# Attention and the last stage in one block, output bias written ahead, loads of the last stage on a new schedule

## The reference

```python
x = L0_attn_x                                    # (4, 2048, 512), f32
# attention: 16 heads of 32, on the normalised x
q = xn @ Wq.T + bq + ocr_bias; k = xn @ Wk.T + bk; v = xn @ Wv.T + bv
scores = einsum('bhsd,bhtd->bhst', q, k) / sqrt(32) + band   # band: 0.1 where |s - t| <= 2
x = x + (softmax(scores) @ v) @ Wo.T + bo
# last stage: both operands of the product go through an fp6 grid, in blocks of 32 along K
out = quantised(layernorm(x)) @ quantised(weight).T + bias
x = x + out
```

## Time and profile before

| | us |
|---|---|
| median of 3 runs | 4258.18 (4256.25 to 4260.35) |
| profiled execution | 4247.55 |
| its span, first to last instruction | 4245.8 |

### The profile page before, as it was taken

The page is one execution under the profiler, slowest core; times in us unless marked ns, Lnnn a source line. Parts: engine busy times, 40 slices in busy tenths (PEclk is TensorE's granted clock), DMA queues, the critical chain, the costliest instruction groups (busy, mean ns, idle before and its releaser), DMA issues. The chain is left out here.

```text
span 4245.8 us, 60060 instructions
## 1 busy us (share of the span) xinstructions
PE 4096.3 (96%) x21392; PEld 2549.3 (60%) x21392; DVE 3324.0 (78%) x5623; ACT 2406.2 (57%) x4652; POOL 3055.4 (72%) x1111
## 2 busy tenths in 40 slices
PE   8999989999999999999999999999999999949999
PEld 6888855555555555555555555555555555417777
DVE  5444449888888888888888888888888888617776
ACT  2222215766766677667666676666766677623221
POOL 2111116888889898989989889888888888935552
PEclk9999988999999999999999999999999999969999
DMA  7666655899999999999999999998999999775442
GB/s 267 207 207 207 207 173 122 182 211 190 202 197 193 201 193 208 187 206 186 212 191 196 198 192 208 186 210 184 210 190 199 195 193 188 160 185 177 160 160 72
DMA packets 283849, 808.30 MB, mean 190 GB/s; under 512 B 28609, under 2 KB 95169, under 8 KB 221122
## 3 DMA queue, kind: packets, MB, share of 16 engines
q0 software_dynamic: 64512, 469.79, 55.7%
q1 hardware_dynamic: 219074, 335.10, 27.1%
HBM read 195.04 MB, written 139.46 MB: 79 GB/s over the span
## 5 line engine op out<-in xcount | busy, mean ns | idle before, releaser
L724 DVE TENSOR_REDUCE part_max<-ps_m 128x1 f32<-128x512 f32 x4096 | 2512.3, 678 | 383.6 <-PE ps_m L625 383.3
L798 POOL TENSOR_TENSOR pair<-p_sb 128x2048 f32<-128x2048 f32 x512 | 2458.1, 4823 | 104.4 <-DVE p_sb L751 58.6
L714 ACT ACTIVATE p_sb<-ps_s 128x512 f32<-128x512 f32 x4096 | 2083.3, 614 | 769.6 <-PE ps_s L644 765.7
L644 PE MATMUL ps_s<-q_st,k_st 97*128 97x512 f32 x4096 | 1687.4, 413 | 6.1 <-DMA q_st<-shift 4.1
L625 PE MATMUL ps_m<-k_st,q_st 96*128 96x512 f32 x4096 | 1643.5, 405 | 20.3 <-POOL k_st L778 20.1
L644 PEld LDWEIGHTS ps_s<-q_st,k_st 97*128 97x128 f32 x4096 | 772.9, 189 | 653.8 <-issue 426.4
L658 PE MATMUL ps_o<-p_sb,v_sb 128*32 128x512 f32 x8192 | 993.4, 602 | 31.2 <-DVE p_sb L751 18.8
L625 PEld LDWEIGHTS ps_m<-k_st,q_st 96*128 96x128 f32 x4096 | 787.3, 192 | 190.9 <-DVE part_max L724 37.6
L658 PEld LDWEIGHTS ps_o<-p_sb,v_sb 128*32 128x32 f32 x8192 | 224.1, 109 | 512.2 <-ACT p_sb L714 320.9
L803 POOL DMA_DIRECT2D pair<-pair x384 | 336.2, 875 | 218.0 <-POOL pair L798 172.5
L172 POOL TENSOR_TENSOR xb<-xin,bo_row 128x2048 f32<-128x2048 f32 x16 | 73.8, 4613 | 418.3 <-DMA xin<-in_x 407.6
(11 more groups left out here) (98 smaller groups left out, 2685.5 us busy)
## 6 DMA issues: line engine op xcount, KB each, us to landing
pair<-pair POOLq DMA_DIRECT2D x448, 1024.0 KB, 8.6
q_st<-q_hi_d SPq DMA_DIRECT2D x128, 256.0 KB, 7.3
k_st<-k_hi_d SPq DMA_DIRECT2D x128, 256.0 KB, 12.2
xin<-in_x SPq DMA_DIRECT2D x16, 1024.0 KB, 8.3
xb_d<-xb SPq DMA_DIRECT2D x16, 1024.0 KB, 5.2
q_hi_d<-s_hi SPq DMA_DIRECT2D x64, 256.0 KB, 2.1
q_lo_d<-s_lo SPq DMA_DIRECT2D x64, 256.0 KB, 2.3
k_hi_d<-s_hi SPq DMA_DIRECT2D x64, 256.0 KB, 2.3
```

The costliest lines, as they stand in the source:

```text
L644: nc.tensor.matmul(ps_s[:, (HG * s + h) % RING_S, :], k_st[0:ROWS + 1, unit // QC % 2, kt // TT, h, kt % TT * P:(kt % TT + 1) * P], q_st[0 ...
L714: nc.scalar.activation(p_sb[:, s % SLOTS, h, :], ps_s[:, (HG * s + h) % RING_S, :], ACT.Exp, scale=SCALE).then_inc(p_ready, 1)
L724: nc.vector.tensor_reduce(part_max[:, unit % 2, col, n:n + 1], ps_m[:, max_place(unit, j) % RING_M, :], AX.X, ALU.max).then_inc(max_taken, 1)
L798: nc.gpsimd.tensor_tensor(pair[:, m % PAIR_RING], p_sb[:, s % SLOTS], p_sb[:, (s + 1) % SLOTS], ALU.add).then_inc(paired, 1)
```

## The change

`attend` and `finish` become one function with one block, `attend_and_finish`. The last stage has no buffers of its own but one (`o_first`): it takes over the tiles of attention as they come free.

- `project`: SP fills the output, chunk by chunk, with the bias of the last product, broadcast from DRAM, behind the stores of v. The product of two rows is gone from `linear`. `res` is now added to the output by a DMA that accumulates; POOL issues it, behind the splits of chunk c, for chunk c - 3.
- Attention: `q_st` has three tiles instead of four, and the queries of unit + 2 are loaded at key tile 1 of each unit. The loads of wo, of o and of the inverses of the first two chunks are spread over the last four units. In the last unit PE projects chunk 0 between the scores (`between_scores`), ACT copies and DVE scales and splits the first two chunks.
- The sum of the last unit's keys is computed, stored, inverted and stored again within the last stage's loop.
- Last stage: `x1` is three tiles, and xb is loaded into them; the inverses have two tiles, one in `pair` and one in `k_st`. SP loads in the order `load_o(c + 2)`, `load_rec(c + 2)`, `load_xb(c + 3)`, and ACT works in the order `high(c)`, `o_highs(c + 2)`, `normalise(c + 1)`. PE's and DVE's orders in the loop are as before.

```diff
@@ project @@
+                sp.dma_start(out_ch[c], ffn_b.unsqueeze(0).unsqueeze(0).to_broadcast([P, TT, D])).then_inc(bias_out, 16)
...
             sp.wait_ge(xb_out, 16 * NCH)
+            sp.wait_ge(bias_out, 16 * NCH)
@@ attend_and_finish @@
-        q_st = sb("q_st", [P, QC, HG, CH], F32R)
+        q_st = sb("q_st", [P, RING_Q, HG, CH], F32R)
...
+        o_first = sb("o_first", [P, NHG, CH])
+        o_hi, o_lo = (k_st[:, 0, 0], q_st[:, 1]), (q_st[:, 2], k_st[:, 1, 0])
+        wo_hi, wo_lo, wd_hi, wd_lo = k_st[:, 0, 2], k_st[:, 0, 3], k_st[:, 1, 1], k_st[:, 1, 2]
+        t_hi, t_lo = k_st[:, 1, 3], q_st[:, 0]
+        x1 = (p_sb[:, 4], p_sb[:, 5], p_sb[:, 0])
+        y, xd, y_q = p_sb[:, 1], p_sb[:, 2], v_sb[:, 0:TT, :].bitcast(FP8)
+        res = (pair[:, 2], pair[:, 3])
+
+        def o_rec(c):
+            return pair[:, 4] if c > 1 and c % 2 == 0 else f32(k_st[:, 0, 1])
+
+        def o_raw(c):
+            return p_sb[:, 3] if c > 1 and c % 2 == 0 else o_first
...
+            def load_o(c):
+                at_least(sp, o_split, NHG * (1 if c == 1 else c - 1))
+                sp.wait_ge(o_out, 16 * ((NHG - 1) * NCH + c + 1))
+                sp.dma_start(o_raw(c)[:], o_by_chunk[c]).then_inc(o_in[c % 2], 16)
+
+            def load_rec(c, gs=range(NHG)):
+                at_least(sp, o_scaled, NHG * (1 if c == 1 else c - 1))
+                if c == 2:
+                    for n in range(CHAINS):
+                        sp.wait_ge(merged[n], 16 * MERGES[n] * NU)
+                sp.wait_ge(rec_out, 16 * (NG - QC + c // QC + 1))
+                for g in gs:
+                    sp.dma_start(o_rec(c)[:, g, :],
+                                 rec_d[g * NCH + c].unsqueeze(1).to_broadcast([HG, HD, CH])).then_inc(rec_in[c % 2], 16)
+
+            def load_xb(c):
+                at_least(sp, res_ready, TT * (c - 2))
+                sp.dma_start(x1[c % 3], xb_d[c]).then_inc(xb_in[c % 3], 16)
...
+                    if 0 < unit < NU - 2 and kt == 1:
+                        sp.wait_ge(scored, HG * KT * unit)
+                        load_q(unit + 2)
...
+                    if unit == NU - 1 and kt == KT - 1:
+                        sp.wait_ge(pv_done, ST - 4)
+                        sp.wait_ge(paired, NM - 2)
+                        load_xb(0)
+            load_xb(1)
...
+            for c in range(NCH):
+                if c + 2 < NCH:
+                    load_o(c + 2)
+                    load_rec(c + 2)
+                if c + 3 < NCH:
+                    load_xb(c + 3)
+                if c == 1:
+                    store_sum(NU - 1)
+                    load_den(NG - 1)
+                if c == 3:
+                    store_rec(NG - 1)
@@ PE @@
+            def between_scores(kt, h):
+
+                t, k = (kt - FIRST_OUT) // 2, (kt - FIRST_OUT) % 2 * 2 + h // 2
+                if h % 2 == 0 or not 0 <= t < TT:
+                    return
...
+                out_part(0, t, k)
...
-                    nc.tensor.matmul(ps_r[:, t, :], ones2[:], fb[:], start=True, stop=False)
@@ ACT @@
+                if unit == NU - 1 and kt == 1:
+                    o_highs(0)
+                if unit == NU - 1 and kt == 10:
+                    o_highs(1)
             copy_o(NU - 1)
-            copy_sum(NU - 1)
+            act.wait_ge(consts2, 1)
+            act.wait_ge(paired, NM)
+            normalise(0)
+            for c in range(NCH):
+                high(c)
+                if c + 2 < NCH:
+                    o_highs(c + 2)
+                if c + 1 < NCH:
+                    normalise(c + 1)
+                if c == 0:
+                    copy_sum(NU - 1)
@@ POOL @@
             def store(c):
-                sp.wait_ge(res_ready, TT * c + TT)
-                sp.dma_start(out_ch[c], res[:, c % 2]).then_inc(out_done[c % 2], 16)
+                pool.wait_ge(res_ready, TT * c + TT)
+                pool.dma_start(out_ch[c], res[c % 2], accum_op=ALU.add).then_inc(out_done[c % 2], 16)
...
+                if c > 2:
+                    store(c - 3)
+            for c in range(NCH - 3, NCH):
+                store(c)
```

More of the change, by code:

```diff
@@ L496, in max_at, with sum_bank @@
         return at // MAXES, at % MAXES
+    def sum_bank(unit):
+        return ps_m[:, sum_place(unit) % RING_M] if unit < NU - 1 else ps_t[:, 0]
     def merges_to(m):
@@ L571, in _ @@
                     if unit > 0:
-                        if kt == SUM_AT + 1:
+                        if kt == SUM_AT + 1 and unit < NU:
                             store_sum(unit - 1)
@@ L675, in burst, with out_part @@
                     add_keys(s // KT - 1)
+            def out_part(c, t, k):
+                if t == 0:
+                    pe.wait_ge(o_split, NHG * c + k + 1)
+                toks = slice(t * P, (t + 1) * P)
+                terms = ((o_hi[c % 2][:, k, toks], wo_hi[:, k, :]), (o_lo[c % 2][:, k, toks], wo_hi[:, k, :]),
+                         (o_hi[c % 2][:, k, toks], wo_lo[:, k, :]))
+                for j, (lhs, rhs) in enumerate(terms):
+                    if c == 0 and t == 0 and k == 0 and j != 1:
+                        pe.wait_ge(wo_in[j // 2], 16)
+                    last = nc.tensor.matmul(ps_r[:, t, :], lhs, rhs, start=(k == 0 and j == 0),
+                                            stop=(k == NHG - 1 and j == 2))
+                if k == NHG - 1:
+                    last.then_inc(out_projected, 1)
@@ L681, in _ @@
                 ahead(1, j)
-            for s in range(ST + SUM_AT + 1):
+            for s in range(ST + 2):
                 for h in range(HG):
@@ new lines, in low, with residual @@
+            def low(c):
+                for k in range(KB):
+                    v.wait_ge(t_hi_done, KB * c + k + 1)
+                    nc.vector.tensor_tensor(t_lo[:, k, :], ps_t[:, k, :], f32(t_hi[:, k, :]),
+                                            ALU.subtract).then_inc(t_lo_done, 1)
+            def residual(c, tiles):
+                for t in tiles:
+                    if t == 0:
+                        v.wait_ge(xb_in[c % 3], 16 * (c // 3 + 1))
+                    v.wait_ge(out_projected, TT * c + t + 1)
+                    nc.vector.tensor_tensor(x1[c % 3][:, t, :], ps_r[:, t, :], x1[c % 3][:, t, :], ALU.add).then_inc(x1_ready, 1)
+                    v.wait_ge(x1_ready, TT * c + t + 1)
+                    nc.vector.bn_stats(stats[:, t, :], x1[c % 3][:, t, :]).then_inc(ln2_steps, 1)
@@ new lines, in scale_o, with o_low @@
+            def scale_o(c):
+                v.wait_ge(o_in[c], 16)
+                v.wait_ge(rec_in[c % 2], 16 * NHG * (c // 2 + 1))
+                for g in range(NHG):
+                    nc.vector.tensor_tensor(o_raw(c)[:, g, :], o_raw(c)[:, g, :], o_rec(c)[:, g, :],
+                                            ALU.mult).then_inc(o_scaled, 1)
+            def o_low(c):
+                for g in range(NHG):
+                    v.wait_ge(o_high, NHG * c + g + 1)
+                    nc.vector.tensor_tensor(o_lo[c][:, g, :], o_raw(c)[:, g, :], f32(o_hi[c][:, g, :]),
+                                            ALU.subtract).then_inc(o_split, 1)
@@ L773, in _ @@
             spread_band(2 * NM - 1)
+            residual(0, range(TT))
+            norm_factors(0)
+            quantise(0, lambda j: None)
+            for n in range(CHAINS):
+                v.wait_ge(merged[n], 16 * MERGES[n] * NU)
+            for c in range(NCH):
+                if c + 1 < NCH:
+                    residual(c + 1, (0, 1))
+                low(c)
+                if c + 1 < NCH:
+                    residual(c + 1, (2, 3))
+                    norm_factors(c + 1)
+                    quantise(c + 1, lambda j: [last_sum(c, t) for t in ((0,), (1, 2), (3,))[j]])
+                else:
+                    for t in range(TT):
+                        last_sum(c, t)
+                if c == 2:
+                    invert(NG - 1)
         @block.gpsimd
         def _(pool):
+            nc.gpsimd.memset(eps2[:], EPS).then_inc(consts2, 1)
+            pool.wait_ge(consts2, 1)
             for i in range(2):
```

469 lines of the change are left out of this document (191 added, 278 removed).

## The result

The changed kernel takes 4375.07 us (median of 4 runs, 4368.07 to 4375.43), the kernel before 4259.27 (4 runs, 4256.25 to 4261.27). The ratio is 1.027, with a 95% interval of 1.025 to 1.029: some 116 us slower.

The account below looks back on a forecast made before the run. PE bounds the kernel before; afterwards a ring of waits paces the last stage. Chunk 0 at 3812, plus 495 for the loop, 4, 21.5, 14 and 10, ends at 4357; on the median 4369, stated as 4368, range 4310 to 4430 us.

Parts of the forecast that it names:

- a ring through SP, POOL, ACT and DVE: Last stage: waits from one chunk's `res` to the next close a circle of 38.1 us a chunk; chance 0.72.
- the landing of the inverses: Last stage: the four loads of inverses land 17.5 us after `res`, using about four of sixteen DMA engines.
- the three last pieces: End of the last stage: chunk 14 takes 21.5 us, chunk 15 takes 14, the last store 10.
- The loop: Last stage, `res(0)` to `res(13)`: 13 periods of 38.1 us, 495 in all.
- collision: Last stage: the accumulating store of the chunk before runs into the next loads, +2 us a chunk, bounds 0 and +5.
- The three orders: Last stage: SP's loads behind xb, ACT's copies before `normalise`, DVE's `res` sums inside `quantise` close the 38.1 us period.
- The handover: Attention to last stage: chunk 0, projected early, is complete at about 3812 us instead of 3863.65.
- The landing of the last fill: End of projections: only the last bias fill of the output is exposed, +3 us, bounds 0 and +6.
- Attention's last unit: 48 output projection products between scores and 8 more ACT copies there cost +8 us, bounds 0 and +16.
- The small parts: Four items: bias product gone (1.7 us a chunk), output fills (+3), three query tiles (0), attention's last unit (+8).
- the rival: Last stage: PE sets the pace at 24.4 us a chunk, 4190 us on the median; chance 0.08.
- The slow clock: Last stage: PE's clock falls each chunk and PE joins the ring, 4420 to 4460 or up to 4508 us; chance 0.15.

Follow-up runs that it names:

- e11: Changed kernel with the output stored by a plain DMA instead of an accumulating one (output lacks the bias): 4369.4 us.
- e1: Changed kernel with SP's load of xb moved behind the loads of o and of the inverses: 4222.03 us, against 4256.02 for the kernel before.
- e2: Changed kernel with ACT's `normalise(c + 1)` put ahead of `o_highs(c + 2)`, SP's order kept: 4311.32 us.
- e3: Changed kernel with the edits of e1 and e2 together: 4250.84 us.
- e8: Changed kernel with the edits of e1, e2 and e4 together: 4231.45 us.
- e5: Kernel before with the inverses loaded by head, 32 rows outermost, nothing else changed: 4239.57 us, against 4249.52.
- e7: Kernel before without its 64 products of the bias (output lacks the bias): 4219.13 us, against 4249.52.
- e6: Changed kernel without the 16 fills of the output and the wait for them (output lacks the bias): 4358.06 us.
- e4: Changed kernel with the inverses loaded by head, 32 rows outermost, SP's and ACT's orders kept: 4290.69 us.
- e9: Changed kernel with the edits of e1 and e4: 4190.55 us (median of 4), against 4257.15, ratio 0.984.

## Why the prediction was right, and where it was wrong

The forecast of 4368 against 4375.07 was right in its mechanism: a ring through SP, POOL, ACT and DVE, with the landing of the inverses as its largest term. That the sum is only 7 us off is luck, since its terms miss by more. At the end of the span, forecast at 4357 and found at 4373.3, `res(0)` is 36 too late, the loop 22 too short, and the three last pieces together 3 too long. And the 10.6 us put between the profiled execution and the median aren't there: the profiled execution of after, 4375.05, is its median.

**The loop** was forecast at 495 us from `res(0)` to `res(13)`, plus 4 for the last keys' sums, and took 477.3. Term by term, in the chunk shown: landing 17.5 and collision 2 against 19.1; scaling 5.0 against 4.93; copy 0.6 as forecast; 13.0 from square root to `res` against 12.0. e11 says how the first two are to be divided: the collision is nothing that shows, and the landing without it is 19. The landing read from the tail in the earlier trace rows was thus some 1.6 us short, and the guess for the collision made it good. The last microsecond is DVE's. In the chunk of before its steps `qs` and `y_q` ran beside other work and took 0.71 and 2.73 (at 4035.20 and 4036.53); in the chunk of after they take 0.20 and 2.29 (at 4097.29 and 4098.11), with POOL and ACT idle. The sums of the last keys cost 2 us at most: the first period is 36.1, the second 38.7, the others 36.6 in the mean.

**The three orders** were named together as one cause. They aren't equal: SP's alone closes the ring (e1), ACT's alone leaves a longer one (e2), and with SP's order mended, ACT's as changed is the better one (e3, e8). That POOL's splits are done before PE wants them held, as the prediction said, but only because the copies ahead of them come early.

**The handover** was forecast to bring chunk 0 to 3812, and it came at 3847.7, 36 late. Four parts:
- Attention starts 19.4 us later than before. Of this 10.2 lie before the v stores, where the fills were to cost nothing. Most of it isn't the change: e5 and e7 have the old projections to the last instruction, and their v stores begin at 602.3 and 601.8; e6, without fills, at 598.3. The profiled execution of before, at 593.1, was a lucky one. By the medians the change costs 116, by the two profiled executions 127.5. I had put the difference to the median down as one lump of 10.6; much of its place is here, as the DVE rows below show for some 3.5 us of it.
- The landing of the last fill: 9.0, forecast 3 with a bound of 6. The mis-sized term is the landing. I took a 1 MB store's 5.2 from SBUF; this one goes from DRAM to DRAM out of one row, and its own row in the DMA view of after says more than twice that, 11.5 (below).
- Attention's last unit: 80.9 us, 59.9 before; forecast +8 with a bound of 16, measured +21. I had counted PE's products and ACT's copies, and no loads.
- From the last store of o to `res(0)` 57.5 us. I let chunk 0 wait for its residual and PE, and overlooked that the ring holds for it too: its last sum stands behind `normalise(1)`, this behind `o_highs(2)`, and these need inverses into a tile of `pair` that the last merges use.

Of the 36 us, the first part makes 10, the second 6 (9.0 for 3), the third 13 (21 for 8), and the last the 6 or 7 that are left.

The rows of these four, in their order. The DVE pass of the first chunk that PE waits for, in before:

```profile
50.16 2.28 DVE L281 TENSOR_TENSOR fw_d<-fw_q,w_qs 128x2048 f32<-128x2048 fp8e4 x1
```

The same pass in after:

```profile
49.91 5.99 DVE L285 TENSOR_TENSOR fw_d<-fw_q,w_qs 128x2048 f32<-128x2048 fp8e4 x1
```

PE behind it in after:

```profile
55.95 3.35 PE L390 MATMUL ps_t<-ident,fw_d 128*128 128x128 f32 x16 [4.07 <-DVE fw_d L285]
```

In before DVE was 0.01 us ahead of POOL's `wo_lo` (50.17), and POOL took 6.71. In after POOL came first, at 48.96 for 4.78, to 53.74, and DVE ended 2.16 us behind that. In e5 and e7, with the instructions of before, the pass took 5.95 and 6.09 too. In all twelve profiles but that of before POOL came first, by 0.2 to 1.3 us, and the pass took 5.94 to 6.48; before's is the exception. PE's work behind it began at 52.50 in before and at 55.95 in after, so this explains some 3.5 of the 10.2 us. Between the v stores of these kernels, 593.1 to 607.6, further differences of this kind are likely, and they weren't followed one by one.

The fill in the DMA view of after (queue, count, KB each, us from issue to landing):

```profile
out_y<-in_ffn_b SPq DMA_DIRECT2D x16, 1024.0 KB, 11.5
```

SP's queue in attention's last unit in after:

```profile
3722.71 7.36 SPq L626 DMA_DIRECT2D k_st<-rec_d  x1
3730.51 4.49 SPq L617 DMA_DIRECT2D o_first<-o_d  x1
```

DVE's scaling of chunk 1 there:

```profile
3767.01 2.50 DVE L1034 TENSOR_TENSOR o_first<-o_first,k_st 128x512 f32<-128x512 f32 x4 [36.52 <-DMA o_first<-o_d]
```

ACT's copies there:

```profile
3767.73 2.43 ACT L908 ACTIVATE q_st<-o_first 128x512 fp32r<-128x512 f32 x4 [14.59 <-DVE o_first L1034]
```

PE there:

```profile
3770.70 0.80 PE L752 MATMUL ps_a<-q_st,k_st 97*128 97x512 f32 x1 [13.44 <-ACT p_sb L922]
```

One issue of inverses holds SP for 7.36 us, the load of o behind it for 4.49, and DVE can scale only 32 us after that. ACT has the copies of chunk 1 in its order ahead of the exponentials, and PE stands 13.44 us for an exponential. In e4 the same scaling began at 3740.20 after 8.90 us of idle time, and 15.1 of the 21 us were gone: the shape of the inverses' loads is the cause of most of this part.

SP's queue at the handover in after:

```profile
3807.93 10.72 SPq L626 DMA_DIRECT2D pair<-rec_d  x4
```

POOL's scaling of chunk 2 behind it:

```profile
3830.36 4.92 POOL L1138 TENSOR_TENSOR p_sb<-p_sb,pair 128x512 f32<-128x512 f32 x4 [21.18 <-DMA pair<-rec_d]
```

3807.93 + 22.4 to the scaling + 5.5 to the square root at 3835.86 + 12.0 to `res` = 3847.8, which is when `res(0)` ends.

**The small parts.** The bias product's price was 0.43 for 0.66 (e7): PE's work is 23.5 a chunk, not 24.4; hidden by the ring, it changed nothing in the time, but it makes the rival better than it was priced. The rival had been put at 4190, and e9 took 4190.55, but that agreement is chance: chunk 0 was done 23 us later than assumed (3835.3 for 3812), chunks were 0.9 shorter, and the 10.6 of the median wasn't there. Chunks 14 and 15 took 22.6 and 14.6 (forecast 21.5 and 14), the last store 11.1 from `res(15)` to the end (10). Three query tiles cost nothing that shows: from the first shift load to the last it is 3031.7 us before and 3033.2 after.

**The slow clock** didn't join the ring. PE stood some 10 us in each chunk. In the one shown the clock was down at 0.50, the 1.2 GHz level, when PE resumed at 4097.43, and the windows have it back at 1.00 from 4102. The Trainium skill ("TensorE: Matmul & The Clock Gate", HAM oscillation) describes a kernel in which each wait for data starts the next tile at the low clock, and the trace agrees that the chunk shown starts slow. But here the clock is back in under 5 us, and the spare time takes it. What it costs shows in PE's busy time only: 186.2 of 260 us (72%, where 65% was forecast), 26.3 a chunk for the 23.5 of e7.

## What to carry to other kernels

When two stages share one queue, list for each load what it waits for, and put loads that wait for the end of a chunk behind those that don't: one such line was worth 153 us here, while the engines' work was the same. A slow transfer that is hidden can come onto the path in every iteration as soon as its issue is tied to a result, so look at its landing, and at how many DMA engines its slowest dimension gives it, before the orders around it are changed. Price a transfer by a row with the same two ends and the same shape, and look for a second execution before a difference of 10 us is charged to the change.

## What the runs showed of the hardware

- A product with two rows, between groups of products with 128, costs 0.66 us of PE's time: its own 0.43, and 0.23 in the group behind it (the earlier trace rows against e7).
- A 1 MB fill from one row of DRAM to DRAM lands in 11.5 us (median, in after); a 1 MB store from SBUF in 5.2.
- DVE's pass with two SBUF inputs (L281, L285) takes 2.28 us, or 5.99 when POOL's has begun first; POOL's four splits take 4.95, or 9.22 in e3, where two such passes of DVE (2.73 and 2.28) run in their time. In the first chunk the pass that began first kept its time and the other was longer, in before by a lead of 0.01 us, in the others by 0.2 to 1.3; PE waited 0.36 us for it in before and 4.07 in after.
- An accumulating 1 MB store from POOL's queue costs 1.25 us of issue and lands in 9.3, against 0.78 and 4.6 for the plain one (e11); the loop loses nothing by it, 36.8 us a chunk against 36.9.
